# The turn from attention to the routed experts, written out by hand on one core

## The reference

```python
h = tok(x)                        # embedding, scan, 4 layers of width 128, head to 64
h = h + attn(layernorm(h))        # linear attention, 4 heads of 32, softmax of q and of k
h = h + ffn(layernorm(h))         # the experts:
#   logits = xn @ Wr + br ; top_vals, top_idx = top_k(logits, 2)
#   w = softmax(top_vals), spread over 8 experts as w_full
#   for e in range(8):
#       y += (gelu(xn @ W1[e] + b1[e]) @ W2[e] + b2[e]) * w_full[..., e]
```

## Time and profile before

| | |
|---|---|
| median of 3 runs | 421.52 us (421.51 to 423.53) |
| the profiled execution's own time | 424.52 us |
| its span, first to last instruction | 422.7 us |
| granted clock of PE, mean | 0.983 of full speed |
| busy share: PE, DVE, ACT, POOL | 93%, 83%, 77%, 61% |

### The profile page before, as it was taken

One profiled execution on the slowest core, in us unless ns is written; L12 is line 12 of the kernel. 1 busy time (PEld: TensorE's weight loads), 2 busy tenths in 40 slices (PEclk: granted clock), 3 DMA queues, 4 the chain that ended last, 5 costly groups with the idle time before them and its releaser, 6 DMA issues.

```text
span 422.7 us, 6309 instructions
## 1 busy us (share of the span) xinstructions
PE 394.7 (93%) x1989; PEld 318.5 (75%) x1989; DVE 352.7 (83%) x850; ACT 324.5 (77%) x555; POOL 259.9 (61%) x389
## 2 busy tenths in 40 slices
PE   4798879999999999999999989999987998999996
PEld 2496568888888888888888869788765775876884
DVE  3887689888988889888988888999976789899885
ACT  1263588999999998888977853678856898888994
POOL 0475787778777879778777557586223643435542
PEclk9999999999999999999999998999996999999999
DMA  6900001212111221232222000000000000000001
GB/s 204 346 2 0 2 21 30 52 51 52 35 40 52 51 47 33 50 51 50 30 47 51 1 0 2 1 3 2 0 2 0 0 2 12 15 12 12 14 12 26
DMA packets 15848, 14.93 MB, mean 35 GB/s; under 512 B 9796, under 2 KB 10568, under 8 KB 15560
## 3 DMA queue, kind: packets, MB, share of 16 engines
q1 hardware_dynamic: 15816, 14.54, 13.6%
HBM read 13.42 MB, written 1.11 MB: 34 GB/s over the span
## 4 chain that ended last, share of the span: by engine, by line
PE 64%; DVE 17%; ACT 12%; issue 4%; POOL 1%; DMA 1%; SPq 0%; POOLq 0%; DVEq 0%; ACTq 0%
PE ps L1449 56%; PE ps L1472 4%; ACT hid L880 3%; ACT w_all L886 3%; ACT ezf L815 2%; DVE hh L1243 2%; DVE hid L1391 1%; DVE stats L960 1%; DVE x L1391 1%; PE ps L1480 1%; DMA xn<-in_w_f 1%; DVE st L1093 1%; DVE kstat L1183 1%; DVE qmax L1195 1%; DVE x L1199 1%
## 5 line engine op out<-in xcount | busy, mean ns | idle before, releaser
L694 ACT ACTIVATE hid<-ps,b_fold 128x512 f32<-128x512 f32 x128 | 84.1, 681 | 21.2 <-PE ps L1449 20.8
L1034 DVE TENSOR_TENSOR hid_lo<-hid,hid_hi 128x1024 fp32r<-128x1024 f32 x64 | 78.8, 1231 | 25.3 <-ACT hid_hi L699 25.1
L1449 PE MATMUL ps<-xn_hi,w_all 128*128 128x512 f32 x256 | 87.4, 402 | 0.6 <-DVE xn_lo L1029 0.6
L1449 PE MATMUL ps<-hid_hi,w_all 128*128 128x512 f32 x256 | 85.0, 393 | 0.0
L699 ACT ACTIVATE hid_hi<-hid 128x1024 fp32r<-128x1024 f32 x64 | 67.9, 1061 | 2.0
L1449 PEld LDWEIGHTS ps<-xn_hi,w_all 128*128 128x128 f32 x256 | 48.4, 189 | 10.8 <-issue 0.9
L1449 PEld LDWEIGHTS ps<-hid_hi,w_all 128*128 128x128 f32 x256 | 48.1, 188 | 9.9
L1449 PE MATMUL ps<-xn_lo,w_all 128*128 128x512 f32 x128 | 50.0, 390 | 0.0
L1449 PE MATMUL ps<-hid_lo,w_all 128*128 128x512 f32 x128 | 49.8, 389 | 0.0
L880 ACT ACTIVATE hid<-ps,eb_fold 128x512 f32<-128x512 f32 x64 | 44.1, 689 | 2.6 <-PE ps L1449 2.2
L1449 PE MATMUL ps<-hid_hi,ew 128*128 128x512 f32 x128 | 42.7, 417 | 1.9 <-ACT hid L880 1.8
(11 more groups left out here) (228 smaller groups left out, 898.6 us busy)
## 6 DMA issues: line engine op xcount, KB each, us to landing
rstd_row<-roots SPq DMA_DIRECT2D x29, 256.0 KB, 4.0
hh<-in_tokens SPq DMA_DIRECT2D x8, 256.0 KB, 7.7
hid<-in_w SPq DMA_DIRECT2D x1, 1024.0 KB, 7.2
rstd_row<-in_w SPq DMA_DIRECT2D x1, 1024.0 KB, 9.9
out<-hh SPq DMA_DIRECT2D x7, 128.0 KB, 2.0
ew_raw<-in_expert_w SPq DMA_DIRECT2D x1, 512.0 KB, 9.4
roots<-rstd SPq DMA_DIRECT2D x29, 2.0 KB, 1.4
ew_raw<-in_expert_w SPq DMA_DIRECT2D x1, 256.0 KB, 9.5
```

Of the source, the lines that this page charges most:

```text
L694: act.activation(hid[:, j % 2, f, :], bank[f], ACT.Gelu, bias=b1_fold[:, j // B * F + f:j // B * F + f + 1]).then_inc(gelu_done, 1)
L1034: dve.tensor_tensor(hid_lo[:, j % 2, 2 * p:2 * p + 2, :], hid[:, j % 2, 2 * p:2 * p + 2, :], hid_hi[:, j % 2, 2 * p:2 * p + 2, :].bitcast( ...
L1449: return pe.matmul(out, lhsT, rhs, start=start, stop=stop)
```

## The change: what it does

Lap -1 is taken out of the loops and written out by hand on PE, ACT and DVE, up to unit 0.

- DVE does the whole routing of group 0 without other work in it; the softmax and masked context of row 7 come behind it, and `scaled_output`, `residual_moments` of row 5 and `scaled_m` of row 7 move into units 1 and 2.
- PE makes `hidden(0)` ahead of row 7's key transposes and `hidden(1..5)` before the first unit; afterwards `hidden(n + LEAD)` with `LEAD = 6` follows `spread_gates(n)`. ACT makes six gelus ahead, in eight buffers (four of them in `x`) where there were four. The hidden banks change places, and row 4's turned input goes to bank 1.
- ACT loads the gelu table directly behind `output_squares(5)`; it stood between row 7's keys and row 6's queries.
- Repeated products whose result nobody reads: two more in lap -2 and 2 + 2 + 2 + 3 in the written-out part (`keep_clock_beside`), where lap -1 had 3 + 3.
- `attend(6)` moves from lap -1 to unit 5, `attend(7)` from unit 7 to 9. The steps of rows 5, 6 and 7 and the routing of groups 1 and 2 are set at single values of `n` from 0 to 42; the four pieces of `ez_of` of a row are split in two pairs.

```diff
-            for m in range(FIRST_LAP, 0):
+            for m in range(FIRST_LAP, -1):
...
+            logits(0)
+            pe.wait_ge(late_weights, 4)
+            hidden(0)
+            keep_clock_beside(2)
+            k_transposes(7, 1)
+            q_transposes(6, 0)
+            pe.wait_ge(kt_ready, B)
+            hidden(1)
+            context(7, 1)
+            hidden(2)
+            keep_clock_beside(2)
+            hidden(3)
+            keep_clock_beside(2)
+            hidden(4)
+            keep_clock_beside(3)
+            pe.wait_ge(qsub_ready, B)
+            turn_gates(0)
+            expert_z_transposes(4, 0)
+            hidden(5)
...
-                if 2 <= n < UNITS:
-                    hidden(n)
...
                     spread_gates(n)
+                if n + LEAD < UNITS:
+                    hidden(n + LEAD)
...
+                if n == E + 5:
+                    expert_z_transposes(5, 1)
+                if n == 2 * E + 1:
+                    logits(1)
+                if n == 3 * E:
+                    expert_z_transposes(6, 0)
+                if n == 4 * E - 1:
+                    expert_z_transposes(7, 1)
+                if n == 4 * E + 3:
+                    logits(2)
```

and on ACT and DVE:

```diff
+            gelu(0)
+            k_turned(7, 1)
+            q_turned(6, 0)
+            gelu(1)
+            gate(0)
+            gelu(2)
+            ez_of(4, 0)
+            ez_hi(4, 0)
+            gelu(3)
+            copy_gates(0)
+            gelu(4)
+            expert_z_turned(4)
+            gelu(5)
...
+                if n + LEAD < UNITS:
+                    gelu(n + LEAD)
...
+                if n == E + 5:
+                    expert_z_turned(5)
...
+                if n == 2 * E + 7:
+                    expert_z_turned(6)
...
+                if n == 4 * E - 2:
+                    expert_z_turned(7)
...
+                if n in (2 * E + 1, 4 * E + 4):
+                    p = 1 if n < 3 * E else 2
+                    take_logits(p)
+                    v = first_max(p)
+                if n in (2 * E + 3, 4 * E + 5):
+                    v = first_hot(p, v)
+                if n in (2 * E + 4, 4 * E + 6):
+                    v = second_max(p, v)
+                if n in (2 * E + 5, 4 * E + 7):
+                    v = second_hot(p, v)
+                if n in (2 * E + 7, 5 * E + 1):
+                    v = weights(p, v)
+                if n in (3 * E, 5 * E + 2):
+                    gates_out(p, v)
```

More of the change, by code:

```diff
@@ L812, in ez_of @@
                     act.wait_ge(ezlo_ready, b - 1)
-                for t in range(NT):
+                for t in tokens:
                     tile = slice(t * D2, (t + 1) * D2)
@@ L886, in hidden_hi @@
                 act.activation(hw_hi[:, slot * S:(slot + 1) * S], hw(slot), ACT.Copy).then_inc(hwhi_act, 1)
+            z_turned(0, 0)
+            z_hi(1, 1)
+            act.preload_act_table(ACT.Exp)
+            z_turned(1, 1)
+            for m in range(FIRST_LAP, -1):
+                a, c, d, e, f = m + 9, m + 8, m + 7, m + 6, m + 5
+                if e >= 0:
+                    output_squares(e, e % 2)
+                if c >= 0:
+                    k_turned(c, c % 2)
+                if d >= 0:
+                    q_turned(d, d % 2)
+                if f >= 0:
+                    ez_of(f, f % 2)
+                    ez_hi(f, f % 2)
+                exp_k(a, a % 2)
+                if a + 2 < B:
+                    z_hi(a + 2, a % 2)
+                if 0 < a and a + 1 < B:
+                    z_turned(a + 1, (a + 1) % 2)
+                copy_v(a, a % 2)
+                if f >= 0:
+                    expert_z_turned(f)
+                exp_q(a, a % 2)
@@ L904, in _ @@
[L904 to L908, removed]
+                if n == 2:
+                    q_turned(7, 1)
+                if n in (4, 8):
+                    copy_gates(n // 4)
+                if n == 5:
+                    output_squares(6, 0)
+                if n in (7, 8):
+                    ez_of(5, 1, pair(n - 7))
+                if n == E + 1:
+                    ez_hi(5, 1)
+                    output_squares(7, 1)
@@ L909, in _ @@
+                if n == 4 * E - 2:
+                    expert_z_turned(7)
+                if n == 2 * E + 5:
+                    gate(1)
+                if n == 5 * E:
+                    gate(2)
+                if u == 5 and 3 <= m < B - 1:
                     copy_gates(m + 1)
@@ L1401, in output @@
-            def output(b):
-                for k, part in enumerate(parts_of_row(b)):
-                    t = slice(part.start // P, part.stop // P)
-                    halves, row = tiles(sum_bank(b, k), P)[:, t, :], tiles(h1[:, b, :])[:, t, :]
-                    dve.wait_ge(yt_done, b + k + 1)
-                    v = own.inc(dve.tensor_tensor(row, halves[:, :, 0:D2], row, ALU.add))
-                    own.wait(v)
-                    dve.tensor_tensor(row, halves[:, :, D2:P], row, ALU.add).then_inc(out_ready, 1)
+            output_sums(5, 1)
@@ L1410, in _ @@
+            take_logits(0)
+            v = first_max(0)
+            v = first_hot(0, v)
+            v = second_max(0, v)
+            v = second_hot(0, v)
+            v = weights(0, v)
+            gates_out(0, v)
+            expert_z_lo(4, 0)
+            masked_context(7, 1)
+            v_total[7] = softmaxes(7, 1)
             for n in range(UNITS + E + 1):
                 m, u = divmod(n, E)
-                if u == 4 and m + 6 < B:
-                    output_sums(m + 6, m % 2)
-                if u == 7 and m + 6 < B:
-                    residual_moments(m + 6, m % 2)
@@ L1416, in _ @@
                 if n < UNITS:
                     dve_job(n)
-                if m in (1, 3):
-                    p = (m + 1) // 2
-                    if u == 2:
-                        take_logits(p)
-                    if u == 3:
-                        v = first_max(p)
+                if n == 1:
+                    scaled_output(5, 1)
+                if n == 2:
+                    residual_moments(5, 1)
+                    scaled_m(7, 1, v_total[7])
+                if n == 6:
+                    output_sums(6, 0)
@@ new lines, in _ @@
+                if n == E:
+                    scaled_output(6, 0)
+                if n == E + 1:
+                    residual_moments(6, 0)
+                if n == E + 2:
+                    expert_z_lo(5, 1)
+                    output_sums(7, 1)
+                if n == E + 5:
+                    scaled_output(7, 1)
+                if n == E + 6:
+                    residual_moments(7, 1)
+                if n == 2 * E + 2:
+                    expert_z_lo(6, 0)
+                if n == 3 * E + 1:
+                    expert_z_lo(7, 1)
@@ L1438, in _ @@
-                if u == 6 and m + 6 < B:
-                    scaled_output(m + 6, m % 2)
-                if u == 5 and m + 5 < B:
-                    expert_z_lo(m + 5, (m + 5) % 2)
                 if 1 <= n <= UNITS and lo_by_dve(n - 1):
```

207 lines of the change are left out of this document (85 added, 122 removed).

## The result

| | before | after |
|---|---|---|
| median of 20 runs | 422.11 us (419.55 to 425.18) | 419.72 us (417.85 to 425.23) |
| the profiled execution, its span | 424.52, 422.7 us | 419.37, 417.6 us |
| granted clock of it | 0.983 | 0.995 |
| ratio after / before | | 0.9947, 95% interval 0.9929 to 0.9965 |

Faster by half a per cent. 411.9 with a range of 408.0 to 417.5 was forecast; the result lies 2.2 us above the range.

What follows compares the result with a forecast made beforehand. PE bounds a bare row, DVE row 2, and group 0's routing holds up the start. Terms -3.8 - 4.6 - 0.4 + 0.3 - 1.1 = -9.6 gave 414.9 from the profiled 424.52, 411.9 against the median 421.52; range 408.0 to 417.5.

Steps and rivals of the forecast that it cites:

- The start, -3.8: Written-out lap -1 up to unit 0: earlier routing brings DVE's first multiply to 318.3 instead of 322.12, -3.8 us.
- Rows 0 to 4 ... -4.6: Rows 0 to 4, each at its busiest engine's pace plus 0.6 for coupling: 59.2 us against 63.8, -4.6.
- row 5's -0.4: Row 5, with the last routing steps on DVE: 10.7 us against 11.08 before, -0.4.
- The base of 63.8: Rows 0 to 4 before, on DVE: 64.25 by first gelu, restated with multiply lags of 1.12 and 0.7.
- slower: Rival, every unit: rounding behind gelu(n+6) loses its 1 us cover; decides from 0.15 us a unit; chance 0.07.
- The new waits of `expert_z_turned`: ACT, rows 6 and 7: waits through a PE unit, up to 1.5 us, cover about 1; bounds 0 to 1 us.
- Row 6, +0.3: Row 6: 10.44 us against 10.04, since PE has no slack left to catch up, +0.3.
- the end, -1.1: Last six units, no hidden or gelu left: DVE's 0.9 sets the pace, six times 0.27, partly given back, -1.1 us.
- The six gelus of lead take one link out of the chain: Rows 0 to 4: a late multiply no longer stops the next gelu, so only 0.6 us is added for coupling.
- The signs: Trace checks: gates near 314.5, multiply near 318.3, clock near 1.00, rows 10, 12, 13, 11, 12, last row under 10.
- moved, not removed: Rival: 4.0 us of DVE work after the gates eats the start's 3.8, leftovers stay coupled; 421 to 422; chance 0.05.
- The leftovers don't run beside each other: Rival: two spread banks couple the engines, rows 1 to 4 stay 51.9, only start and row 0 gain; 415.4; chance 0.20.

Runs made afterwards that it cites:

- the run with repeated products alone: Kernel before plus eight repeated products between hidden(1) and the turn of group 0's gates: median 421.20 us, ratio 0.9979; its profiled execution had clock 0.998.
- both edits: Changed kernel, gates of rows 5 and 6 turned two units later and ACT's rounding of unit n-1 ahead of gelu(n+6): median 415.51 us, ratio to before 0.9863.

## Why the prediction was wrong

**The start, -3.8: right.** It measured -4.12, and 0.72 of that comes from before the changed part (`logits(0)` starts at 305.73, not 306.45; in the run with repeated products alone, whose code is the same up to there, it starts at 304.41). So the part itself won 3.40, and 2.81 against the kernel before at full clock. Set off by the 0.72, every step lies within 0.3 us of its forecast, the multiply 0.4 late: `hidden(0)` 307.52 for 308.24, key transposes 308.54 for 309.2, `hidden(1)` 310.08 for 310.8, PE through at 315.18 for 315.8, the copied gates 315.81 for 316.45, spread 317.49 for 317.95, multiply 318.00 for 318.3. PE waits 0.40 and 0.78 (forecast 0.5 and 0.7) and the clock is full. The table load costs nothing: it ends at 307.69, and the gelu behind it starts 0.57 us later, on PE's product. A drain of 1380 ns behind the load, as the Trainium skill (ScalarE: Activation LUTs, What ACT_TABLE_LOAD costs) has it, would have put that gelu at 309.1; the trace disagrees.

**"Rows 0 to 4 ... -4.6": this is the step that failed**, and with it row 5's -0.4. By first multiply rows 0 to 4 went from 65.05 to 63.14 us, -1.9, and row 5 from 10.05 to 11.54, +1.5; against the kernel before at full clock rows 0 to 4 won nothing (62.94). Forecast were 80.3 us for rows 0 to 6 (59.2 + 10.7 + 10.44); they took 85.08. (The base of 63.8 was 1.2 too low: row 5's first multiply stood 1.92 behind its gelu, not 0.7. Row 5's own base of 11.08 was too high by about as much.) Of the 4.8 us the runs show, with 3.4 for the first two together:
- 1.8, the two early turns. "The gates of row 6 come out on DVE in unit 42 and PE turns them in 44, two units of cover" counted units as if both engines stood in the same one; PE is up to three ahead, so there was no cover left. The other turn's wait, for DVE to take group 2's logits, was not in the prediction.
- 1.8, the rounding behind the gelu. That was the mechanism of the rival "slower", with 0.03 us a unit on average (1.8 / 56), far from the 0.15 from which it would have decided. It showed in row 0 above all and partly by pushing DVE onto POOL.
- 1.4 that no edit removed (81.69 with both, the sum of that version's rows): row 3 takes 12.19 for 11.1, row 0 10.82 for 10.0, row 5 11.20 for 10.7, the rest about even. The method, each row its busiest engine and 0.6 for coupling over five rows, is short by that. It put rows 0 to 2 and 4 on DVE, and its estimates for PE add up to 76.1 us. In the trace of the version with both edits PE is busy for 79.8 of the 81.7, and in rows 1 and 4 for all but 0.04, DVE for less; in row 1 ACT, which the forecast of the rows doesn't price, is busy throughout as well (columns as above):

```profile
327.61:339.84 12.23, 12.19 (x61) 9.54 (x60) 11.47 (x40) 12.23 (x27) 8.25 (x11) 1.00 0.01 2
365.31:377.24 11.93, 11.93 (x60) 9.90 (x61) 11.39 (x29) 11.19 (x21) 5.78 (x5) 1.00 0.05 11
```

  That points to PE's rows as priced too low; no experiment tried it, and why row 3 is slow stays open.

**The new waits of `expert_z_turned`**, 0 to 1 us for rows 6 and 7, lie within their bounds: in the trace of the kernel after ACT waits 0 for row 6's transposes and 0.36 us for row 7's. What they cost in time was not separated from that rest.

**The base of the forecast.** "The profiled execution took 424.52, so 414.9 by its own measure; it lay 3.0 over the median 421.52. Against the median: 411.9." By its own measure the kernel after took 419.37, which is 4.5 over; the other 3.0 come from this sentence. The clock of row 0 (0.83) and row 2 (0.88) was read as part of the kernel, and getting it back was part of -4.6. But executions of the kernel before have clocks from 0.982 to 1.000, and the profiled one was among the low ones. A sum that wins back what this execution lost can't be taken off a median whose executions had lost less. From the logits' start to the end the profiled execution of before took 116.25 us (422.7 - 306.45), the kernel before at full clock, with eight repeated products, 113.59 (418.0 - 304.41), the changed kernel 111.87 (417.6 - 305.73). So of 4.4 us the clock is 2.7 and the change 1.7: the start wins 2.81 (15.08 to 12.27), the end 0.96 (15.48 to 14.52), and the seven rows lose 2.05 (83.03 to 85.08). With both edits they win 1.34. The fastest executions agree: 419.6 to 419.9 us at clocks of 0.998 to 1.000 before, 417.8 to 418.1 at 0.999 after. The prediction had priced the low clock of row 0 at 2.5 and that of row 2 at 1.5; the first cost 1.1 (start and row 0, 29.03 to 27.91), the second 1.6 (rows 2 and 3, 25.56 to 23.97).

**Row 6, +0.3, and the end, -1.1:** +0.36 and -0.92, right. But the end's gain is what the lead gives back of its own price. "The six gelus of lead take one link out of the chain" was wrong; a lead of two has the same rows.

**The signs** were right: faster, at full clock, gates out at 313.94, first multiply before 320, rows 1 and 2 together 25.78, under the 27 named, and the last row shorter than 10 (its multiplies end at 410.91, 7.8 behind 403.08). Rows 0 and 4 broke the named pattern of 10, 12, 13, 11, 12. Of the rivals "moved, not removed" (421 to 422) lay nearest in time, though outside the range, and at full clock the rows did eat 2.05 of the start's 2.81. But that was no loss that the moved work must bring: with two orders changed the rows win. "The leftovers don't run beside each other" (415.4) had the rows right, 51.9 us for rows 1 to 4 where they took 51.29, but its cause, the two spread banks, was the smaller one: PE waits 1.29 us for them in rows 0 and 1 (0.78 and 0.51), and 3.19 for two turns that were placed too early.

## What to carry to other kernels

Where engines run apart by some units, count a step's cover in the time of the engine that waits: one of them may stand three units further on at the same moment, and two units of cover on paper were a stop of 1.73 us. Before a clock loss in a profile is counted as something to win, look at how far the clocks of the other executions lie apart, and take the sum and its base from the same clock. Lead and repeated work should be tried each by itself: of the changed kernel's parts the lead cost 0.6 to 0.8 us net, and the repeated products, with two units of lead, stood in a wait that was there anyway and held the clock behind it. A gain of one or two us is read from the changed part onward at the same clock: what lay ahead of it moved by more than that from one execution to the next.

## What the runs showed of the hardware

- The same idle time of PE, 1.46 us at the same place, was followed by a clock of 1.00 in one execution and of 0.57 for 3 us in another. The clock of a kernel is a spread of values, not one.
- In twelve executions of the changed kernel the time ran from 417.77 us at a clock of 0.999 to 421.31 at 0.990: 0.4 us for each 0.001. The kernel before, with 419.6 at 1.000 and 422.9 at 0.982 on one chip, lost half as much. Straight lines through all their recorded executions give 0.3 and 0.2.
- Some instructions of DVE that met one of POOL's ran nearly behind it, whichever came first, and others not at all. In DVE's timeline of the kernel after, 1296 took 1.54 us (0.43 at 315.31) and 1375 took 0.69 (0.22 for the same size elsewhere):

```profile
346.55 1.54 DVE L1296 TENSOR_TENSOR ew_raw<-ezf,ew_raw 128x256 fp32r<-128x256 f32 x1
...
385.12 0.69 DVE L1375 CAST w_all<-scratch 128x128 fp32r<-128x128 f32 x1
```

  and in POOL's, beside them:

```profile
346.53 1.29 POOL L616 TENSOR_TENSOR w_all<-x,w_all 128x512 fp32r<-128x512 f32 x1
...
383.95 1.78 POOL L616 TENSOR_TENSOR w_all<-x,w_all 128x512 fp32r<-128x512 f32 x1 [1.59 <-ACT w_all L868]
```

  The second of POOL's is itself held: DVE's `hidden_lo` had started at 383.92, took its usual 0.69, and POOL 1.78 for 1.29. But the multiply (1384), which has one of its inputs in PSUM, is never held: 21 of the 64 start while such a subtraction of POOL's runs, and none takes over 0.69 us. The Trainium skill (GPSIMD Engine Reference, 1. Specifications) names instructions of DVE with two inputs in SBUF, as 1296, and those in a 2-port performance mode. The trace agrees for the first kind, with 1.54 us for 0.43. 1375 has one input, so that it would be of the second; no run here shows its mode.
- The table load of 1.28 us had nothing behind it that a trace shows: the next instruction began at its end in the kernel before, and 0.57 us later, on PE's product, in the kernel after.
